# A wait for all gathers in flight at every eighth tile, in two layers of a graph network on one core

## What is computed

```
# layer 0 (aggregation of x[src], mean, two linear maps)
x = layernorm(x + x @ w_self.T + b_self + mean_over_edges(x[src]) @ w_neigh.T + b_neigh)
# layer 1: an MLP on every edge, mean per destination, an MLP on every node
h = relu(concat(x[src], edge_attr) @ W1 + b1) @ W2 + b2
x = layernorm(x + mlp(concat(x, scatter_mean(h, dst), u)))
# layer 2: sums over edges, no gather of rows in the kernel
x = layernorm(x + relu((x_comb + segment_sum(x_comb[src], dst)) @ W1 + b1) @ W2 + b2)
# layer 3: attention with four heads over the edges
e = exp(leaky(a_src[src] + a_dst[dst]) - seg_max[dst])
x = layernorm(x + relu(layernorm(segment_sum(h[src] * e, dst) / denom + bias) * gamma + beta))
```

## Time and profile before

| | us |
|---|---|
| median of 3 runs (6285.25 to 6294.11) | 6291.95 |
| the profiled execution, its span | 6290.0 |
| TensorE matmuls busy in it | 4549.5 (72%) |
| TensorE weight loads | 3664.1 (58%) |
| VectorE | 2674.4 (43%) |
| ScalarE | 1822.6 (29%) |
| GpSimd | 3113.1 (49%) |

### The profile page before, as it was taken

The page is one execution under the profiler, slowest core; times in us unless marked ns, Lnnn a source line. Parts: engine busy times, 40 slices in busy tenths (PEclk is TensorE's granted clock), DMA queues, the critical chain, the costliest instruction groups (busy, mean ns, idle before and its releaser), DMA issues.

```text
span 6290.0 us, 72860 instructions
## 1 busy us (share of the span) xinstructions
PE 4549.5 (72%) x24017; PEld 3664.1 (58%) x24017; DVE 2674.4 (43%) x9938; ACT 1822.6 (29%) x3934; POOL 3113.1 (49%) x3324
## 2 busy tenths in 40 slices
PE   6999978888888898888989995344444444544445
PEld 5888855666666566666669994234444343434334
DVE  8999943333333333333335442233333333333334
ACT  5888842222222222222224552011111111111112
POOL 0000036666666666666640004666666666666663
PEclk9999989999999999999999997666666666666667
DMA  6777765555555555555647784122222222222221
GB/s 152 166 163 167 164 162 178 178 179 177 180 176 179 179 177 179 179 179 177 182 133 220 244 243 112 44 48 48 47 47 48 49 48 47 47 50 48 48 48 29
DMA packets 473053, 804.93 MB, mean 128 GB/s; under 512 B 73183, under 2 KB 301706, under 8 KB 462698
## 3 DMA queue, kind: packets, MB, share of 16 engines
q0 software_dynamic: 140192, 443.73, 28.3%
q1 hardware_dynamic: 318378, 346.76, 18.1%
q10 hardware_dynamic: 14112, 9.74, 0.5%
HBM read 663.72 MB, written 136.22 MB: 127 GB/s over the span
## 4 chain that ended last, share of the span: by engine, by line
PE 47%; another core or an unknown queue 25%; DVE 12%; issue 11%; DMA 2%; ACT 2%; POOL 1%; DVEq 0%; ACTq 0%
PE bank L1034 12%; PE bank L1021 10%; PE bank L1205 7%; PE bank L689 5%; PE bank L669 3%; PE bank L1523 2%; DVE ring L987 2%; DVE ring L1415 2%; DMA atab<-at 2%; PE bank L1487 1%; PE bank L590 1%; POOL ring L550 1%; DVE hs L638 1%; PE bank L970 1%
## 5 line engine op out<-in xcount | busy, mean ns | idle before, releaser
L550 POOL DMA_INDIRECT ring<-ptab,src x1612 | 1526.9, 947 | 854.7 <-issue 446.2
L550 POOL DMA_INDIRECT ring<-htab,src x1612 | 1526.5, 947 | 853.1 <-issue 448.3
L1034 PE MATMUL bank<-ring,oh 128*126 128x384 f32 x3224 | 1257.8, 506 | 30.8 <-issue 30.3
L987 DVE TENSOR_TENSOR ring<-bank,ring 128x512 f32<-128x512 f32 x806 | 543.0, 687 | 1613.4 <-remote 855.2
L1021 PE MATMUL bank<-w1e,ea 128*128 128x256 f32 x3224 | 892.4, 400 | 252.2 <-DVE ring L987 190.9
L1021 PEld LDWEIGHTS bank<-w1e,ea 128*128 128x128 f32 x3224 | 620.1, 199 | 541.1 <-issue 270.9
L1523 PE MATMUL bank<-ring,oh 128*126 128x132 f32 x3224 | 675.6, 357 | 337.0 <-DVE ring L1415 224.6
L1003 ACT ACTIVATE ring<-ring 128x1024 f32<-128x1024 f32 x403 | 425.6, 1056 | 1400.5 <-DVE ring L987 1112.6
L1523 PEld LDWEIGHTS bank<-ring,oh 128*126 128x126 f32 x3224 | 583.5, 252 | 424.0 <-issue 219.9
L1034 PEld LDWEIGHTS bank<-ring,oh 128*126 128x126 f32 x3224 | 624.7, 196 | 290.5 <-issue 74.8
L689 PE MATMUL bank<-xhl,at 128*126 128x258 f32 x3822 | 712.6, 323 | 0.0
(11 more groups left out here) (268 smaller groups left out, 4727.0 us busy)
## 6 DMA issues: line engine op xcount, KB each, us to landing
atab<-at POOLq DMA_DIRECT2D x78, 1543.5 KB, 9.9
ring<-ea_r SPq DMA_DIRECT2D x403, 256.0 KB
ea<-ea_t SPq DMA_DIRECT2D x403, 256.0 KB
adjb<-atab SPq DMA_DIRECT2D x156, 535.5 KB, 4.6
adjb<-atab SPq DMA_DIRECT2D x78, 472.5 KB, 4.5
ring<-ptab,src POOLq DMA_INDIRECT x1612
ring<-htab,src POOLq DMA_INDIRECT x1612
ptab<-pO ACTq DMA_DIRECT2D x49, 128.0 KB, 7.3
```

The lines of the kernel that those rows point to most:

```text
L550: return e.indirect_dma_start(o, None, table, bass.IndirectOffsetOnAxis(ap=src[:, t:t + 1], axis=0))
L987: e.tensor_tensor(group1(gi, m % 2), MLP[m % 3][:, :].rearrange("p (g f) -> p g f", g=2), group1(gi, m % 2), ALU.add).then_inc(s_edge, 1)
L1034: w = e.matmul(SUM[s % 2][0:SL, 0:384], slots_of(s, i), rv1[:, t // G % NR1, t % G, :], start=i == 0, stop=t == END[s])
```

## The change

Before the first gather of every second group of layer 1 GpSimd waits for `landed1(gi - 1)`, the landing of the group issued just before; in layer 3 it waits before tiles 8 and 16 of a group until the tiles of this group issued so far have landed (the full value less 16 for each tile still to come). Either way nothing that it has issued is on its way any more when it goes on. In layer 1 that makes 201 waits, one every eight tiles, in layer 3 155 (78 at tile 8, 77 at tile 16), with 8 tiles between them inside a group and 13 across a boundary of two groups of 21.

```
@@ -834,6 +834,8 @@
                 for gi in range(NG):
                     if gi >= NR1:
                         e.wait_ge(s_sum1, G * (gi - NR1 + 1))
+                    if gi and gi % 2 == 0:
+                        e.wait_ge(*landed1(gi - 1))
                     for j in range(G):
                         gather(e, rv1[:, gi % NR1, j, 0:256], ptab[:, :], gi * G + j).then_inc(landed1(gi)[0], 16)
 
@@ -1241,6 +1243,9 @@
                     for i in range(SIZE[s]):
                         if s >= NR3 and i % G == 0:
                             e.wait_ge(s_sum3, START[s - NR3] + min(i + G, SIZE[s - NR3]))
+                        if i == 8 or i == 16:
+                            r, n = landed3(s)
+                            e.wait_ge(r, n - 16 * (SIZE[s] - i))
                         gather(e, rv3[:, s % NR3 * GT + i, :], htab[:, :], START[s] + i).then_inc(landed3(s)[0], 16)
```

## The result

The changed kernel takes **6455.69 us** (median of 4 runs, 6448.08 to 6463.48) against 6293.03 us (4 runs, 6285.25 to 6296.05) before, a ratio of 1.0267, 95% interval 1.0249 to 1.0286. It is **slower by 2.7%**; I had forecast 6155 us, and even my range ended at 6330. The profiled execution of the changed kernel has a span of 6461.4 us, 171.4 over the one before.

What follows compares the result with a forecast made beforehand. The prediction took GpSimd's gathers to be stopped by held-up semaphore news, not GpSimd's own pace, to bound the kernel. Layer 1 +10 and layer 3 −145 us made −135 from 6290.0, giving 6155 us, range 6075 to 6330.

Steps and rivals of the forecast that it cites:

- What bounds the kernel: Gathers of layers 1 and 3: GpSimd stopped 352 and 349 us because back-to-back gathers hold up news of the engines' semaphores.
- The price of a new wait: GpSimd, from last issue's end until rows land: 1.75 us in layer 1 (+352 us), 1.22 in layer 3 (+189 us).
- Stops that go: GpSimd's old stops at waits for the sums, no longer needed after the new waits: −352 us and −349 us.
- remaining stops: GpSimd still stops sometimes for updates held during a run's last gathers: +25 us in layer 1, +30 in layer 3.
- Sum: All terms together: layer 1 +10 us, layer 3 −145 us, together −135 us against the profiled 6290.0 us.
- the ends: After the last gathers of layers 1 and 3, other engines stand close behind GpSimd: 15 us off each, bounds 0 and 30.
- rival 2: Layer 1: last gathers always land among SP's loads, 2.8 us a wait; +66 us in all, 6355 us; chance 10%.
- Can the other engines follow?: Layer 3: engines need 27.3 us a group against GpSimd's 28.3; layer 1: TensorE 2067 us against 2367; they keep up.
- rival 3: Layer 3 follows half way, engine crossings meeting held updates: about 29.5 us a group, some 85 us given back, 6240 us; 13%.
- Costs them nothing until GpSimd's lead is used up: VectorE and ScalarE wait for gathers 20 to 80 tiles after landing, so one late by 2 us costs them nothing.
- Rival 1: GpSimd's waits for the sums: new waits end too early, many old stops remain; +249 us, 6540 us; chance 12%.
- The rule against the change: The skill's advice to issue DMAs early and wait late; taken alone it would add 541 us and give 6831 us.

Runs made afterwards that it cites:

- the third chip: Another chip, where both kernels ran again unchanged and with profiles: the kernel before took 5537.38 us, the changed kernel 6462.68 us.

## Why the prediction was wrong, by its own steps

- **What bounds the kernel: right for that chip, and only for it.** The stops of 352 and 349 us were there; the changed kernel has none of them, and the kernel before is 754 to 757 us faster on four other chips, with no such stop in the one trace taken of it there. That they go with late starts of the other engines while gathers go out is read from the traces. That a row of gathers holds the news up, and a drain lets it through, fits but is not shown. For it: the late starts and the missing records occur almost only beside gathers, and with the drains the late starts are gone in layer 1 and come to 100 us instead of 237 at L564. Open is whether the drain does it, or GpSimd's slower pace alone; some late starts remain with 8 or 13 gathers between two drains. That chip did not come back; fewer drains on it, or pauses of the same length without a drain, would have told.
- **The price of a new wait: this is the step that failed.** I took 1.75 us (bounds 1.4 and 2.8) and 1.22 (1.2 and 1.5); it is 2.83 and 2.21, outside both. That a wait costs no 0.30 us on top, and that GpSimd starts again in 0.25 (it is 0.26), was right. The landing was right in layer 3, 1.26 us, and too low in layer 1: 2.02, near the 2.1 of the earlier trace rows, where my 1.75 stands on a landing of 1.8. Two terms were missing, that is, put at nothing without a reason. One is the 0.33 us from the last packet to the record of the semaphore: I took the silence of the queue for the moment at which GpSimd is freed. The other is the 0.5 us for the second wait, though the rows of the order show the two semaphores on one gather. Per wait, as idle time: 1.26 + 0.33 + 0.76 = 2.35 us in layer 3, against a median of 2.36, and 2.02 + 0.34 + 0.76 = 3.12 in layer 1, against 3.15. Of the 370 us that the waits cost too much, some 200 are the second wait (99 + 98), 120 the news, and 44 layer 1's landing (201 × 0.22).
- **Stops that go:** all 701 us, as I said. Of the 55 us that I had left for remaining stops 12 came, and at other places.
- **Sum:** for layer 1 I had +10 us and it is +228 for its gathers; for layer 3 −145 and it is −4 (the ends, 22 and 29 us, apart). The whole: 370 us too much for the waits, less 43 at the remaining stops and 21 at the ends, is 306, and 6461.4 − 6155 = 306.
- **Two slips in the numbers.** My forecast's own bounds (1.4 us a wait, no remaining stops, 30 us at each end) take off 70 + 55 + 30 us and give 6000, not 6075; and rival 2 is 10 + 211 − 145 = +76, 6366, not +66. Neither would have brought the result into the range.
- **"Can the other engines follow?"** They could. In layer 3 they were said to need 27.3 us a group, and GpSimd came to 2363.7 / 78 = 30.3 us a group by its waits alone. So rival 3 (layer 3 only half way) did not occur either: its 29.5 us a group lay nearer by luck, its mechanism did not hold.
- **"Costs them nothing until GpSimd's lead is used up":** it is used up all the time. VectorE waits 1732.8 us for layer 1's gathers. With GpSimd as the bound, each microsecond of a drain is a microsecond of the kernel.
- **The ends:** 22 us between the layers and 29 behind the last gather, where I took 15 each. Right in mechanism; the bound of 30 held.
- **Rival 1 (the old stops stay)** did not occur: they went. Its 6540 us lies nearer to the result than my forecast, by luck. **Rival 2 (dear landings in layer 1)** had the nearest price, 2.8 us a wait, but for another reason: not the landing (2.02), but landing, news and a second wait. And it left layer 3 untouched, where the same terms cost as much again, 155 × (2.2 − 1.22) = 152 us.
- **The rule against the change.** On the first chip 911 + 12 us stood against 701 us of stops, and the rest, +222, less 51 at the ends, is the result. On the others nothing stood against it, and the waits are the whole story: 5535.71 + 924.6 (580.5 + 344.1 of the table) = 6460 us, measured 6462.68. The rule of the Trainium skill, DMA: Bandwidth & Descriptors, Rules for kernel authors (issue early, wait late) points that way, and the runs agree. The same page, under Anatomy of one DMA, gives about 2.0 us for the fixed part of a DMA issued from GpSimd, setup and completion together. From the end of the issue to the last record the trace has 1.6 us in layer 3 and 2.4 in layer 1, and from the start of the issue, 0.95 us earlier, 2.5 and 3.3.

## What to carry to other kernels

A drain on the engine that sets the pace costs the landing, plus the news, plus the start, plus one more step if the same instruction waits for something else, each time; take the sum from a stop that the trace shows whole, from the last instruction before to the first after, and not from the moment when the queue falls silent. If a wait must be, let one transfer stay under way (1.31 instead of 2.39 us here, and 0.30 instead of 1.59), and put it on an instruction that has no other wait. And before mending waits that no instruction explains, look whether the trace has its records of the semaphores, and whether another chip or another time shows these waits: here the kernel before was 754 to 757 us faster on four others.

## What the runs showed of the hardware that I had not expected

- The same program takes 6285 to 6296 us on one chip and 5533 to 5542 on four others, each time over several runs and without overlap. Of the 754 us between the two traces 708 lie in the stretches where GpSimd's gathers go out back to back, and 46 right behind them (18 between the layers, 28 at the end); layer 0 and the gathers themselves (0.947 us) are alike. In the same stretches the first chip's trace lacks about three quarters of the semaphores' records. Cause open.
- The record of a landing comes 0.33 us after the last packet's end. A stopped GpSimd needs 0.26 us from that record to the next gather, and 0.76 if that gather has two waits, while a wait already met costs nothing, even as an instruction of its own (5535.75 against 5537.29 us with 344 of them).
- Landing after a run of gathers is 1.26 us after the end of the issue in layer 3 whatever the run, and 1.48, 2.14 and 2.26 us in layer 1 after 4, 8 and 16 gathers.
- Without the stops TensorE is granted its full clock throughout layer 1, 1.00 or 2.4 GHz, where the earlier trace rows has a mean of 0.94, and TensorE is busy with the same work for 1962 us instead of 2067. The changed kernel, whose TensorE waits at every drain, has 0.94 on the third chip too, so this goes with the pauses and not with the chip.
